# A decoder layer of 32 batches on one core: each engine's loop marked at its top with a hint that the jump at its end will be taken

## The reference

```python
x = x + attn(layernorm(x), Wq, Wk, Wv, Wo)                       # 16 heads of 64, rotary q and k
x = x + xattn(layernorm(x), ctx, mask, Wq, Wkv, Wout, bout)      # 16 heads, keys and values from ctx
x = x + ffn(layernorm(x), Wg, We, be)                            # 8 experts, top 2, all experts computed
```

## Time and profile before

| | |
|---|---|
| median of 3 executions | 3658.52 us |
| the profiled execution | 3660.11 us |
| its span, first to last instruction | 3658.2 us |
| mean granted TensorE clock | 0.993 |
| TensorE busy | 3508.1 us, 96% |
| VectorE, ScalarE, GpSimd busy | 64%, 61%, 58% |

### The profile page before, as it was taken

One profiled execution on the slowest core, in us unless ns is written; L12 is line 12 of the kernel. 1 busy time (PEld: TensorE's weight loads), 2 busy tenths in 40 slices (PEclk: granted clock), 3 DMA queues, 4 the chain that ended last, 5 costly groups with the idle time before them and its releaser, 6 DMA issues.

```text
span 3658.2 us, 87217 instructions
## 1 busy us (share of the span) xinstructions
PE 3508.1 (96%) x28992; PEld 2956.4 (81%) x28992; DVE 2357.1 (64%) x7401; ACT 2232.2 (61%) x6442; POOL 2123.2 (58%) x1928
## 2 busy tenths in 40 slices
PE   5999999999999999999999999999999999999997
PEld 4788888888888888888888888888888888888886
DVE  6666666666666666666666666666666666666665
ACT  5656566665565665666655655656666566556563
POOL 5555666555665556665556655566655566555661
PEclk8999999999999999999999999999999999999999
DMA  3100000000000000000000000000000000000000
GB/s 96 37 10 12 13 7 10 10 12 12 7 12 11 10 12 11 9 10 10 12 12 7 10 10 13 12 10 10 10 10 12 12 7 10 10 12 12 10 9 7
DMA packets 46845, 48.23 MB, mean 13 GB/s; under 512 B 8256, under 2 KB 43328, under 8 KB 46400
## 3 DMA queue, kind: packets, MB, share of 16 engines
q1 hardware_dynamic: 45696, 41.99, 3.9%
q10 hardware_dynamic: 704, 0.27, 0.0%
HBM read 33.86 MB, written 8.39 MB: 12 GB/s over the span
## 4 chain that ended last, share of the span: by engine, by line
PE 44%; issue 33%; POOL 16%; DVE 4%; ACT 2%; POOLq 0%; DMA 0%; ACTq 0%; DVEq 0%
PE unit_ps L537 10%; POOL probs L1147 10%; PE oT_ps L666 7%; PE pT_ps L649 7%; PE score_ps L633 7%; PE unit_ps L525 5%; PE wo_ps L691 4%; POOL rope L1159 2%; POOL swap L1155 2%; POOL q_both L1136 1%; ACT probs L800 1%; PE unit_ps L556 1%; DVE neg_max L928 1%; POOL rstd L1123 1%; PE unit_ps L547 1%
## 5 line engine op out<-in xcount | busy, mean ns | idle before, releaser
L1147 POOL TENSOR_TENSOR probs<-probs,inv_sum 128x512 f32<-128x512 f32 x1024 | 1062.1, 1041 | 1007.6 <-DVE inv_sum L922 1006.6
L789 ACT ACTIVATE pT<-pT_ps 128x512 f32<-128x512 f32 x1024 | 608.8, 596 | 146.8 <-PE pT_ps L649 144.6
L800 ACT ACTIVATE probs<-probs,neg_max 128x256 f32<-128x256 f32 x1024 | 510.9, 502 | 268.9 <-DVE probs L939 268.9
L649 PE MATMUL pT_ps<-ident,probs 128*128 128x128 f32 x4096 | 637.9, 281 | 11.1 <-POOL probs L1147 10.7
L649 PEld LDWEIGHTS pT_ps<-ident,probs 128*128 128x128 f32 x4096 | 452.8, 141 | 224.2 <-issue 152.6
L800 ACT ACTIVATE probs<-score_ps,neg_max 128x256 f32<-128x256 f32 x1024 | 477.9, 477 | 218.6 <-DVE neg_max L928 218.6
L666 PE MATMUL oT_ps<-pT,v_sb 128*64 128x256 f32 x4096 | 560.8, 395 | 4.5 <-ACT pT L789 4.1
L939 DVE TENSOR_SCALAR_CACHE_REDUCE probs<-score_ps,mask_add 128x256 f32<-128x256 f32 x1024 | 433.3, 479 | 104.2 <-PE score_ps L633 102.3
L537 PE MATMUL unit_ps<-xs_hi,w_lo 128*128 128x256 f32 x1536 | 460.5, 300 | 9.2 <-DVE swap L973 7.7
L537 PE MATMUL unit_ps<-xs_hi,w_hi 128*128 128x256 f32 x1536 | 436.7, 284 | 0.0
L537 PE MATMUL unit_ps<-xs_lo,w_hi 128*128 128x256 f32 x1536 | 436.3, 284 | 0.0
(11 more groups left out here) (121 smaller groups left out, 8528.0 us busy)
## 6 DMA issues: line engine op xcount, KB each, us to landing
x_in<-dram_x SPq DMA_DIRECT2D x32, 256.0 KB, 2.7
xn<-dram_ctx SPq DMA_DIRECT2D x32, 256.0 KB, 2.7
layer_out<-x SPq DMA_DIRECT2D x32, 256.0 KB, 2.2
swap<-dram_bout SPq DMA_DIRECT2D x32, 128.0 KB, 3.0
rope<-dram_be SPq DMA_DIRECT2D x32, 64.0 KB, 2.8
rope<-dram_we SPq DMA_DIRECT2D x5, 256.0 KB, 2.7
probs<-dram_sk SPq DMA_DIRECT2D x4, 256.0 KB, 4.3
x<-dram_cq SPq DMA_DIRECT2D x4, 256.0 KB, 3.1
```

The lines of the kernel that those rows point to most:

```text
L649: last = nc.tensor.transpose(pT_ps[s % 2][:, k * T + t * P:k * T + (t + 1) * P], probs[:, hs % P_BUFS, t, k * P:(k + 1) * P], ident[:])
L789: nc.scalar.activation(flat(pT[:, s % 2, :, :]), pT_ps[s % 2][:], ACT.Copy).then_inc(pT_ready.sem, 1)
L800: last = nc.scalar.activation(dst, src, ACT.Exp, bias=neg_max[:, h % STATS, t:t + 1], scale=1.0 if h < H else -1.0, accum_out=row_sum[:, h ...
L1147: nc.gpsimd.tensor_tensor(weights, weights, inv.unsqueeze(2).to_broadcast([P, NT, T]), ALU.mult).then_inc(probs_ready.sem, 1)
```

## The change

The loop of `bodies` is opened through the general call, for the one engine, with the option that marks the loop's top with a hint. The option adds one instruction to each engine at the start of every pass; it names the compare-and-branch at the end of the pass and says that it is likely taken. The loop's bounds, its body and its register are the same.

```diff
--- before.py
+++ after.py
@@ -440,7 +440,7 @@
 
             body(-1)
             body(0)
-            with engine.Fori(1, B - 1) as b:
+            with nc.Fori(1, B - 1, engines=[engine.engine], hint_back_edge=True) as b:
                 body(b)
             body(B - 1)
             body(B)
```

## The result

The changed kernel takes 3600.21 us (median of 4 runs, 3599.12 to 3600.84) where the kernel before took 3658.98 us (4 runs). The ratio is 0.9839, with a 95% interval of 0.9821 to 0.9856. The forecast was 3599.0 us in a range of 3592 to 3610. The profiled execution has a span of 3597.3 us, 60.9 us less than before.

A forecast was written before the change was run, and what follows sets the result against it. TensorE was taken to bound the kernel, stalling at each taken loop jump while code is fetched. Gap 50.3 plus clock 10.2 minus 1 for the last pass gives 59.5 us won: 3599.0 us, range 3592 to 3610.

The forecast's parts named there:

- term 1: TensorE's waits before a batch's first score matmul, 29 times behind the taken jump, go: 50.3 us won.
- term 2: Six 3.4 us stretches of TensorE at half clock, each just after a taken jump, all go: 10.2 us won.
- term 3: Later in the batch, TensorE is not held up again by the VectorE, ScalarE, slot 2 scores chain: nothing taken back.
- term 4: The added hint instructions on each engine's pass are covered by other work: 0 us, at most 1.5 us.
- term 5: Last pass, hinted for a jump not taken, may miss its next block once: 1 us lost, bounds 0 and 3.5.
- the fetch near 479 us: TensorE's last fetch before the jump, read as the unused block behind it; the hint would make it the loop's first block.
- the sign that was named: TensorE's compare-and-branch at the loop's end would last near 80 ns, 30 times.
- B: Hint without effect, never acted upon or its block pushed out before the jump: 3658.5 us; chance 0.06.
- C: Only TensorE's jump mended; VectorE still late, TensorE waits 1.05 us in slot 2: 3628 to 3639 us; chance 0.05.
- D: Slower: hint steers the next fetch at once, TensorE's second block missing early in each pass: 3710 to 3720 us; chance 0.04.

The follow-up runs named there:

- dve_only: Kernel before with the hint on VectorE's loop alone; 3659.9 us, ratio 0.9995.
- pe_dve: Kernel before with hints on TensorE's and VectorE's loops, none on ScalarE, GpSimd and SyncE; 3599.8 us, ratio 0.9829.
- pe_slot34: Changed kernel with TensorE's hint moved from the loop's top to the start of slot 34, other hints at the top; 3602.0 us.
- pe_head239: Changed kernel, all five hints, with TensorE's loop begun at slot 239 of a code block, so it touches 9 blocks, not 8; 3638.6 us.
- pe_head200: Changed kernel, all five hints, with TensorE's loop begun at slot 200 of a code block, so it touches 9 blocks, not 8; 3650.2 us.
- pe_late: Changed kernel with TensorE's hint moved from the loop's top to the start of slot 35, other hints at the top; 3617.5 us.

## Why the prediction was right

**The gap (term 1, 50.3 us)** was read off the waits and off the one jump not taken. It went entirely: no wait of 29 times is left. **The clock (term 2, 10.2 us)**: all six stretches are gone. The two terms gave 60.5 us for the loop and the passes show 61.9. The missing 1.4 us I can't place. It may be that the gap was taken as idle time: at the jump of the earlier trace rows that is 1.69 us, where the difference from start to start is 1.77. How many stretches there are is partly chance: 6 of 29 jumps before, 5 in dve_only with nearly the same waits (48.4 us).

**Nothing comes back (term 3)** held: a pass is 109.80 us, and the exponentials of slot 1 still end 0.2 us ahead of the scores of slot 2. **The hints (term 4)** last 31 to 39 ns each. By pe_dve those on the other three engines cost nothing in the time. **The last pass (term 5, 1 us)**: the tail grew by 2.2 us, inside the bounds of 0 and 3.5, but not by what was priced. The term took a stall of TensorE; TensorE's wrong hint cost nothing, and VectorE's, which the term leaves out, cost 1.3 us. The other 0.9 us fall to the clock at the end by inference only, and the head, which no term covers, gave 1.2 us back. So a part of the closeness of 3600.2 to 3599.0 us is luck.

**How the hint works** was told otherwise than it came. The prediction had the fetch near 479 us turned to the loop's first block, which would land 7 us ahead of the jump. In the changed kernel there is no fetch at all in the passes, so the first block must still have been in store. A fetch in time would have done as well: pe_slot34 has one and the same pass, 109.81 us. The number did not hang on it, since the untaken jump gave the price of a jump without a stall, whatever removes the stall. The compare-and-branch also lasts 216 ns, not the 80 of the sign that was named; the 80 ns belong to the untaken one.

**The rivals.** B, no effect, fell with the compare-and-branch of 216 ns. The Trainium skill ("Runtime: NRT & Kernel Launch", Instruction fetch mechanics) calls prefetch purely sequential: the runs disagree for a hinted jump. In pe_slot34 a fetch begins 1.9 to 5.1 us ahead of the jump and the jump doesn't wait, and in the changed kernel 261 packets fewer were fetched and the branch took 216 ns. C was the right account of a kernel that the change wasn't, to within 0.12 us a pass. It also shows why the change names all engines: with TensorE's hint alone half of the gain is lost. D did not come; a stall at the place that it names was made in pe_head239, by other means.

**What was not foreseen** is how little the change hung on the hint's time of arrival, and how much on the blocks. The prediction left open whether the fetches would stay at 283 or vanish. They vanished, and the counts say why: nine blocks a pass, one of them in vain, became eight. With nine blocks of its own, in the two places tried, the same line brought passes of 111.07 and 111.45 us (pe_head239, pe_head200), 25 and 14 us less than before over the 29 passes and not 62.

## What to carry to other kernels

Count the taken jumps of a loop and look for a wait of that number on any engine, whatever releaser it names; a jump that falls through in the same trace prices the mend. Hint all engines whose code doesn't stay in store, since the second one's stall is hidden only as long as the first one's lasts, and put the hint at the loop's top. How many blocks a loop touches, how deep the jump lies in its block and how much of the first block is left behind the head decided the rest here. All three hang on where the loop lies, so an edit ahead of the loop may move them.

## What the runs showed of the hardware

- TensorE's instruction fetches are 16 KB packets: 9 in each pass of 1931 instructions before, 10 at slot 200 without a hint, none in the changed kernel, where by the count 8 blocks suffice. VectorE and ScalarE fetch 8 KB packets on one queue, and stalled only where by the count the loop touches four blocks and has no hint.
- A taken jump out of store took TensorE's sequencer 3.3 to 3.9 us before, of which 1.5 to 2.0 us reach the matmuls. From the jump to the start of the fetch it is 0.9 to 1.5 us, and a fetch takes 0.9 to 1.5.
- With the hint near the jump, the fetch that it steers began 3.1 us (pe_late) or 2.0 to 5.2 us (pe_slot34) behind it. With the hint at the top and nine blocks it began some 4.1 to 5.3 us behind the entry of the jump's block in pe_head200, and 0.5 us behind it in pe_head239. Without a hint at slot 200 the fetch of the next block began 1.9 to 2.5 us ahead of the jump in 24 of 30 passes.
- A gap of 1.5 to 2.0 us on TensorE was followed by 3.4 us at the lower clock in 6 of 29 jumps before. In pe_late, with gaps of 0.4 to 0.9 us, it never was.
